# One wait for three pieces, or three waits: the last matrix product of a two-layer gated block on one Trainium2 core

## The reference, cut to what matters

```python
x = x + tanh(g_xattn[0]) * L0_xattn(ctx, ctx, layernorm(x), ssm_kernel, D)   # long convolution, per head
x = x + tanh(g_ffn[0])   * L0_ffn(layernorm(x), router, gate, up, down)      # routed, 8 groups of 176
x = x + tanh(g_xattn[1]) * L1_xattn(layernorm(x), ctx, mask)                 # softmax(x ctx^T / 16) ctx
x = x + tanh(g_ffn[1])   * L1_ffn(layernorm(x), w_fc, w_proj)

def L1_ffn(x, w_fc, w_proj):          # w_fc is 640 x 256, w_proj 256 x 640, both made ternary
    h = einsum('bsd,hd->bsh', x, ternary(w_fc))
    h = square(relu(h))               # 640 inner values a row
    return einsum('bsh,dh->bsd', h, ternary(w_proj))
```

## Time and profile before

| | us |
|---|---|
| median of 3 executions | 263.65 |
| lowest, highest | 262.89, 264.14 |
| the profiled execution's own time | 263.31 |
| its span (first to last instruction) | 261.6 |
| PE busy in the span | 232.4 (89%) |
| DVE busy | 184.8 (71%) |
| ACT busy | 109.7 (42%) |

### The profile page before, as it was taken

One profiled execution on the slowest core, in us unless ns is written; L12 is line 12 of the kernel. 1 busy time (PEld: TensorE's weight loads), 2 busy tenths in 40 slices (PEclk: granted clock), 3 DMA queues, 4 the chain that ended last, 5 costly groups with the idle time before them and its releaser, 6 DMA issues.

```text
span 261.6 us, 4679 instructions
## 1 busy us (share of the span) xinstructions
PE 232.4 (89%) x1606; PEld 221.0 (84%) x1606; DVE 184.8 (71%) x514; ACT 109.7 (42%) x222; POOL 82.8 (32%) x125
## 2 busy tenths in 40 slices
PE   6395979878689999999999989999999999999973
PEld 6384978777578998998989889999899999998972
DVE  1447999998986889777999385563584753786663
ACT  0501335652103346273727655453542572363241
POOL 3559698257699530100073200100020100111110
PEclk9859899999959999999999999999999999999996
DMA  5599247000000005000000000000001001000100
GB/s 164 131 355 261 88 137 222 3 1 0 4 0 0 0 3 200 3 1 0 3 0 3 0 0 4 0 4 0 0 3 40 3 0 40 4 0 0 43 21 20
DMA packets 14038, 11.50 MB, mean 44 GB/s; under 512 B 2912, under 2 KB 13760, under 8 KB 14016
## 3 DMA queue, kind: packets, MB, share of 16 engines
q1 hardware_dynamic: 13920, 11.16, 14.1%
q10 hardware_dynamic: 96, 0.05, 0.2%
HBM read 10.14 MB, written 1.07 MB: 43 GB/s over the span
## 4 chain that ended last, share of the span: by engine, by line
PE 53%; DVE 19%; POOL 10%; issue 8%; DMA 4%; ACT 4%; DVEq 0%; POOLq 0%; ACTq 0%
PE bank L691 18%; PE bank L541 11%; PE bank L548 6%; PE bank L760 4%; POOL fold L1307 4%; POOL kv L1296 3%; PE bank L746 3%; PE bank L694 3%; DVE prod L1021 2%; POOL fold L1310 2%; DMA x_res<-in_x 2%; DMA toe<-lag_rows 2%; PE bank L732 2%; DVE act L1188 2%; PE bank L592 2%
## 5 line engine op out<-in xcount | busy, mean ns | idle before, releaser
L691 PE MATMUL bank<-w_split,xt 128*128 128x352 f32 x384 | 68.8, 328 | 0.0
L691 PEld LDWEIGHTS bank<-w_split,xt 128*128 128x128 f32 x384 | 61.3, 188 | 0.3 <-issue 0.2
L1270 POOL TENSOR_SCALAR ve<-mv 128x2 f32<-128x2 f32 (+2 forms) x16 | 3.6, 226 | 141.1 <-DVE mv L978 141.1
L1188 DVE SCALAR_TENSOR_TENSOR act<-silu,scal,bank 128x176 f32<-128x176 f32 x64 | 22.5, 393 | 17.4 <-ACT silu L883 16.6
L541 PE MATMUL bank<-d_split,a_t 128*128 128x256 f32 x264 | 33.7, 285 | 0.0
L541 PEld LDWEIGHTS bank<-d_split,a_t 128*128 128x128 f32 x264 | 32.2, 191 | 0.3 <-DVE a_t L938 0.2
L1307 POOL TENSOR_TENSOR fold<-prod 128x256 f32<-128x256 f32 x32 | 25.2, 787 | 12.2 <-DVE prod L1025 11.9
L883 ACT ACTIVATE silu<-bank 128x352 f32<-128x352 f32 x32 | 14.9, 465 | 29.2 <-PE bank L694 29.1
L592 PE MATMUL bank<-kv,toe 128*128 128x160 f32 x64 | 17.7, 363 | 10.0 <-POOL kv L1296 4.5
L592 PEld LDWEIGHTS bank<-kv,toe 128*128 128x128 f32 x64 | 11.9, 225 | 12.4 <-issue 7.5
L769 ACT ACTIVATE a_t<-bank 128x384 fp32r<-128x384 f32 (+1 forms) x32 | 14.7, 460 | 17.8 <-PE bank L548 17.7
(11 more groups left out here) (140 smaller groups left out, 437.1 us busy)
## 6 DMA issues: line engine op xcount, KB each, us to landing
toe<-lag_rows SPq DMA_DIRECT2D x4, 512.0 KB, 5.9
ring<-in_down_p SPq DMA_DIRECT2D x2, 704.0 KB, 5.1
x_res<-in_x SPq DMA_DIRECT2D x2, 512.0 KB, 4.8
ctx<-in_ctx_rows SPq DMA_DIRECT2D x2, 512.0 KB, 5.2
ring<-in_gate_p SPq DMA_DIRECT2D x2, 512.0 KB, 8.7
ring<-in_up_p SPq DMA_DIRECT2D x2, 512.0 KB, 4.1
out_x<-x_res SPq DMA_DIRECT2D x3, 256.0 KB, 2.2
tern_w<-in_w_fc SPq DMA_DIRECT2D x1, 640.0 KB, 4.3
```

The source lines that it names most:

```text
L691: pe.matmul(psum((name, b, c))[:, 0:CW], lhs, w_split[:, w, kt, part, cols], start=i == 0, stop=False)
L1188: drain(dve.scalar_tensor_tensor(out=act[:, g * NI:(g + 1) * NI], in0=silu[:, n % 2, cols], scalar=scal[:, b, g:g + 1], in1=psum(("up", b, ...
```

## The change

PE's wait for all three pieces, which stood ahead of the whole `out` step, is taken away. Three waits stand in its place, inside the loop over the tiles of the unit's first batch: for one piece before tile 0, for two before tile 2, for three before tile 4. The second batch of a unit has none. The bank's `claim` now comes ahead of the waits. Number and order of the matmuls stay as they were, and so do all other engines' programs.

```diff
@@ -752,10 +752,11 @@
                     if u == 0:
                         for k in range(3):
                             wait_drained(pe, ("turn_proj", k))
-                    pe.wait_ge(hid_lo, 3 * (u + 1))
                     claim(pe, step)
                     for k in range(len(UNITS[u])):
                         for j in range(JT):
+                            if k == 0 and j % 2 == 0:
+                                pe.wait_ge(hid_lo, 3 * u + j // 2 + 1)
                             for part in range(2):
                                 last = pe.matmul(psum(step)[:, k * L:(k + 1) * L],
                                                  hid_t[:, j, part, k * P:(k + 1) * P],
```

## The result

Fifteen executions of each kernel give 260.99 us after and 262.47 us before as medians (259.40 to 262.59 and 261.23 to 264.14). The ratio is 0.9942, with a 95% interval of 0.9916 to 0.9969: 1.5 us faster, between 0.8 and 2.2. The kernel before came out 1.2 us lower than the median of the three executions that the forecast had (263.65).

A forecast was written before the change was run, and what follows sets the result against it. PE bounds the whole, busy 89% of the span, but the edit gains only at two waits on the path. 1.66 + 0.25 - 0.1 = 1.8 us takes the 263.65 us median to 261.8, range 260.9 to 262.8.

The forecast's parts named there:

- two of five: Of five out steps, only those of units 3 and 4 waited for `hid_t`, 2.3 us in all; only these gain.
- Unit 4: Last out product: matmuls start piece by piece, so its end moves from 258.96 to 257.30, 1.66 us.
- last pair: Unit 4's last two out matmuls: start at 256.80 as before and end at 257.30, taking 0.50 us.
- tail: From DVE's last low part to its last update in unit 4: shrinks from 2.24 us to about 0.6.
- first four matmuls: Unit 4's out product: need only piece 0, start 0.05 us after its release, at 255.22, and end at 255.96.
- The clock: Unit 4's out product: 0.70 of the 1.66 us is PE's fall to 1.2 GHz, which the last pair no longer meets.
- Rival A: Clock doesn't fall at the end in the executions that count: gain 1.1 us in all, 262.5; chance 0.22.
- Unit 3: Out step starts 0.28 us earlier, its third wait hidden; `x1t` limits what follows; ceiling 0.28, floor zero, taken 0.25.
- Rival B: Only one of two waits pays: unit 3's head start is eaten by `x1t`; gain 1.55, 262.1 us; chance 0.15.
- The met waits: Eight added waits in units 0 to 3, met when PE arrives: 0.01 us each, 0.1 in all.
- The sum: 1.66 + 0.25 - 0.1 = 1.8 us: profiled execution from 263.31 to 261.5, median from 263.65 to 261.8.
- range: Forecast time between 260.9 us (no cost of waits, earlier clock fall) and 262.8 us (no clock fall, some offset).

The follow-up runs named there:

- unit 4 alone: Kernel before with piece-by-piece waits only in unit 4's out step: 260.59 us against 262.84, ratio 0.9933.
- units 0 to 3 alone: Kernel before with piece-by-piece waits in units 0 to 3, one wait in unit 4: 262.35 us against 262.84, ratio 0.9982.
- filler runs: Kernel before with 13 or 7 constant matmuls ahead of unit 4's one wait, `claim` ahead of the wait in every unit: ratios 0.9995 and 0.9968.
- run of two waits: Kernel before with two waits a unit, for two pieces ahead of tile 0, the third ahead of tile 4: 261.89 us in one execution against 262.78.
- 30 added: Kernel before with ten further, long-met waits in each out step of units 0 to 2: 262.96 us in one execution against 262.78.
- second timing: The changed kernel, otherwise unedited, timed again on another chip against the kernel before: 259.44 us against 262.64, ratio 0.9853.
- high-then-low order: Kernel before with out matmuls piece by piece, high parts waiting for ACT, then low for DVE: 259.37 us, ratio 0.9885; again 260.49, 0.9887.

## Why the prediction was right

**Which waits matter.** The forecast took two of five, and both were there. The runs split them: unit 4 alone has a ratio of 0.9933, units 0 to 3 alone 0.9982, with an interval that takes in 1; by the lengths it is 1.64 and 0.26 us.

**Unit 4: 1.66 us forecast, 1.64 in the profile pair.** The last pair took the 0.50 us forecast for it and the tail was 0.60 as forecast. One inner step was off without effect: the first four matmuls began 0.15 us after their piece (255.48 to 255.63), not 0.05, and piece 1 came later anyway. Most of that is `claim`, of which the forecast said that it costs nothing; ahead of an unmet wait it costs 0.07, as the filler runs show in unit 3. As a value for all executions the term was a little small: with tails of 2.24 to 2.60 before, it is 1.64 to 2.00, since the one profile that I had showed the mildest fall of the five.

**The clock, 0.70 of it.** Right in kind: filling the wait keeps 1.00 and takes the product from 2.14 to 1.46. Rival A, with 0.22 the strongest beside the forecast, was wrong. What misled me was that PE kept 1.00 through the idle time of unit 3. The two places are not alike: at the end, with 1.80 us of idle time ahead of the product, the clock fell in all five profiles with one wait and no filler; with 1.25 us there, in the run of two waits, it stayed at 1.00; in unit 3, with 1.2 us, it fell in one of fourteen. One figure of that rival was misread too: not half of the ten matmuls' time lay under the low clock, but 1.71 of 2.16 us (257.25 to 258.96), which left less room for an earlier fall. The Trainium skill ("TensorE: Matmul & The Clock Gate", Part 1) says that the moment of a change moves from run to run; the trace agrees as to the moment, which lay between 0.25 us before the product's start and 0.45 after it (the latter from 256.80 to 257.25 in the first profile), but for this wait it never moved out of the way.

**Unit 3: 0.25 forecast, 0.26 measured** (1.70 to 1.44), with `x1t` the limit, as named. Rival B would have had nothing there.

**The met waits: 0.1 forecast, nothing measured**, at 30 added.

**The sum** for the profiled kernel was 1.8 us and it measured 1.90 in the two places. The median was 260.99 where I said 261.8, not through the gain but through the base, which was 262.47 over 15 executions and not 263.65 over three: 1.18 us too high. The gain came out 0.3 smaller in the timing (1.5 us), which took back a part of that. The median lies only 0.09 us above the lower end of the range (260.9), so that the time fell inside it owes something to luck; the mechanism does not.

## What to carry to other kernels

Where a step waits once for several pieces made one after the other, and it is the last work on the path, let it take them piece by piece: the gain is up to the work on all but the last piece (0.96 us here at the full clock, 1.46 less 0.50), and a wait between matmuls that is already met cost PE nothing in any row here. What stands right ahead of an unmet wait is not free: the bank's `claim` there cost 0.07 us. A wait that keeps PE idle (1.8 us here) can cost twice, by itself and by the lower clock behind it; the pieces brought both back here. Where the engine found its pieces ready, as in units 0 to 2, the same edit is worth nothing.

## What the runs showed of the hardware that I had not expected

The granted clock in earlier stages moves the time more than this change does. Among the first 15 executions of the changed kernel, the three with a mean clock of 0.980 took 259.40 to 259.55 us, and the three with 0.960 or 0.961 took 261.99 to 262.59. One stretch of low clock at 151 us put the profile after back by 1.6 us (from 1.13 ahead to 0.49 behind). To this I put down that two timings of one kernel gave 0.9942 and 0.9853, with intervals that don't meet: the six executions of the second all had 0.979 or 0.980. The profile of the second timing bears it out. Its granted clock was 1.00 from 148 to 156 us, and unit 0's out step, the first that the change touches, began there at

```profile
192.36 2.55 PE L761 MATMUL bank<-proj_t,hid_t 128*128 128x256 f32 x20
```

against 194.91 in the profile after: 2.55 us of the 2.56 between the two executions (259.43 and 261.99) lie ahead of it. Why that timing had fewer such stretches is open. The kernel before was no faster beside it (262.64 us, against 262.47), and the high-then-low order, on the same chip, had 0.967 to 0.980. The two lengths inside the profile repeat within 0.01 us for a given form of the waits at the full clock, which is why they carry nearly every verdict here. What sets how many such stretches an execution has was not tried.
